# A mixture layer behind a state-space scan on one core: batch 0's output projection, norm and routing moved into batch 1's scan, expert weights loaded by expert

## The reference

```
h = layernorm(x) * (1 + ca) + sa
x = x + ga * (mamba(h) @ Wout.T + bout)       # 512 channels, 16 states each
h = layernorm(x) * (1 + cb) + sb
x = x + gb * moe(h)                           # 8 experts, the 2 best of each token

# mamba, for each channel, state and time step:
hs = exp(delta * A) * hs + (delta * u) * B
y  = sum over the 16 states of hs * C;  y = (y + u * D) * silu(z)
# moe, for each token and each of its two experts:
out += weight * (silu(h @ w0[e]) * (h @ w1[e])) @ wo[e]
```

## Time and profile before

| | us |
|---|---|
| median of three runs | 856.41 (855.0 to 859.22) |
| the profiled execution, its own time | 857.02 |
| its span, first to last instruction | 855.1 |
| TensorE busy | 736.4 (86%) |
| DVE busy | 637.4 (75%) |
| GpSimd busy | 512.8 (60%) |
| ACT busy | 329.6 (39%) |

### The profile page before, as it was taken

The page is one execution under the profiler, slowest core; times in us unless marked ns, Lnnn a source line. Parts: engine busy times, 40 slices in busy tenths (PEclk is TensorE's granted clock), DMA queues, the critical chain, the costliest instruction groups (busy, mean ns, idle before and its releaser), DMA issues. The chain is left out here.

```text
span 855.1 us, 10146 instructions
## 1 busy us (share of the span) xinstructions
PE 736.4 (86%) x2245; PEld 362.4 (42%) x2246; DVE 637.4 (75%) x880; ACT 329.6 (39%) x364; POOL 512.8 (60%) x266
## 2 busy tenths in 40 slices
PE   5899998878888878879788887896499999999994
PEld 3444343222233322323233332575256666666663
DVE  4478899999999999999899998577435445445442
ACT  1786956456454545445354444011111111111110
POOL 1013234999999999899999999546522222222222
PEclk9999999999999999989999899997699999999998
DMA  9354645867668577567689898196323322322220
GB/s 291 99 144 154 206 153 146 207 172 190 178 158 212 158 187 196 160 172 188 171 198 249 217 232 212 56 382 247 105 71 61 50 38 40 49 43 41 46 29 0
DMA packets 61731, 126.33 MB, mean 148 GB/s; under 512 B 11338, under 2 KB 33290, under 8 KB 61580
## 3 DMA queue, kind: packets, MB, share of 16 engines
q1 hardware_dynamic: 49908, 116.12, 49.2%
q0 software_dynamic: 7152, 8.48, 5.6%
q10 hardware_dynamic: 4648, 1.48, 0.7%
HBM read 98.08 MB, written 24.69 MB: 144 GB/s over the span
## 5 line engine op out<-in xcount | busy, mean ns | idle before, releaser
L1450 POOL TENSOR_TENSOR pool<-pool,hT 128x1024 f32<-128x1024 f32 x128 | 298.8, 2357 | 23.0 <-PE PS L619 23.0
L619 PE MATMUL PS<-pool,ident 128*128 128x512 f32 x512 | 267.8, 648 | 44.9 <-POOL pool L1450 43.7
L907 ACT ACTIVATE PS<-pool,negA 128x1024 f32 (+1 forms) x128 | 143.1, 1118 | 188.2 <-DVE pool L1167 188.2
L619 PEld LDWEIGHTS PS<-pool,ident 128*128 128x128 f32 x512 | 95.9, 200 | 158.8 <-POOL pool L1450 81.4
L1520 POOL DMA_INDIRECT out<-uT,ptab x39 | 60.5, 1552 | 168.1 <-DVE uT L1396 161.5
L741 PE MATMUL PS<-pool,uT 128*128 (+1 forms) x312 | 143.5, 603 | 0.6 <-issue 0.6
L1167 DVE TENSOR_TENSOR_SCAN pool<-PS,pool 128x1024 f32<-128x1024 f32 x64 | 142.9, 2272 | 0.4 <-ACT PS L907 0.4
L601 PE MATMUL PS<-pool 96*128 96x512 bf16 x256 | 79.6, 393 | 23.4 <-DVE wz_sb L1155 13.4
L1370 DVE TENSOR_TENSOR uT<-uT,PS 128x512 f32<-128x512 f32 x39 | 26.9, 689 | 88.3 <-PE PS L741 85.5
L1167 DVE TENSOR_TENSOR_SCAN pool<-PS,spread 128x1024 f32<-128x1024 f32 x32 | 73.1, 2284 | 13.2 <-POOL spread L1470 8.9
L1470 POOL TENSOR_TENSOR spread<-spread,pool 128x1024 f32<-128x1024 f32 x32 | 75.4, 2356 | 12.4 <-ACT spread L913 12.4
(11 more groups left out here) (176 smaller groups left out, 782.5 us busy)
## 6 DMA issues: line engine op xcount, KB each, us to landing
hT<-C_scratch SPq DMA_DIRECT2D x128, 512.0 KB, 5.3
pool<-in_w SPq DMA_DIRECT2D x16, 512.0 KB
uT<-expert_in_scratch SPq DMA_DIRECT2D x39, 130.5 KB
Y<-Y SPq DMA_DIRECT2D x32, 128.0 KB, 2.4
C_scratch<-Y SPq DMA_DIRECT2D x8, 512.0 KB, 2.6
pool<-du_scratch SPq DMA_DIRECT2D x8, 512.0 KB, 6.0
Y<-in_wo SPq DMA_DIRECT2D x8, 512.0 KB
expert_in_scratch<-zrow SPq DMA_DIRECT2D x16, 130.5 KB, 5.6
```

What stands on the lines that cost most here:

```text
L619: m = pe.matmul(PS[:, 6 + half, :], ident[:, :], prod[:, k % PR, HF * half:HF * half + HF], start=False, stop=k == DS - 1)
L907: act.activation(pair(2 * (k % 2)).unsqueeze(1), delta[:, bass.ds(g2 * 2 + r, 1), :], ACT.Exp, scale=decay[:, bass.ds(g2 * (2 * DS) + n, 1 ...
L1450: gp.tensor_tensor(prod[:, k % PR, :], hst[:, k % HR, :], crep[k % RC], ALU.mult).then_inc(prod_done, 1)
```

## The change

- **Batch 0 inside batch 1's scan.** The last two pairs of chunks are written out on all engines. In chunk 5 TensorE runs the projection of tiles 0 to 3 in steps 0 to 3, where its `back` stood, and in chunk 6 that of tiles 4 to 7 (`blocks_behind`); the `back`s follow from step 4, two and one in turn. The projection uses the PSUM pair of the sums, and a fifth matmul adds x itself. ACT takes the tile out in steps 4 to 7 (`take_x2`), DVE measures it behind the scans of steps 7 to 10 (`among_scans`), GpSimd computes the power and the shift behind step 11, ACT normalises (`normal_x2`), TensorE turns tiles forward and back in steps 0 to 4 of chunk 7, and ACT scales and shifts them there and copies the rows (`take_turned`, `take_rows2`). The gate logits of the eight tiles stand ahead of the last three `back`s.
- **Products.** From step 72 of 128 the ring of products has `PW` = 6 buffers.
- **Routing groups.** They are eight tiles, four and four. Batch 0 is one group, picked straight behind the last scan.
- **Loads.** w1 of experts 4 to 6 is loaded in the last pair of chunks. Behind the scan the order is w0, w1, wo of one expert after the other, and TensorE waits for the weights of two experts at a time. Batch 0's part of x is stored in chunk 7.
- **First slots.** TensorE's first eight slots are written out, with the expert as a constant.

```diff
-NQ = 4
-TQ = NT // NQ
+TQ = 4
+GROUPS = ((0, NTB), (NTB, NTB + TQ), (NTB + TQ, NT))
+NQ = len(GROUPS)
+S1 = NG // 2 * DS
+RING = S1 + 8
...
+PW = 6
...
+        prods = [prod[:, 0, :], prod[:, 1, :], delta[:, CH - 1 + NG // 2, :], szT[:, 1, :], szT[:, 2, :], szT[:, 3, :]]
...
+        def prod_at(n):
+            return prods[n % PR] if n < RING else prods[(n - RING) % PW]
...
-                        if last and k in (3, 7, 11):
-                            w0_of(3 * r + k // 4)
+                        if last and (r, k) in ((0, 3), (0, 7), (1, 7)):
+                            w1_early(CH + 2 * r + k // 4 - r)
+                        if last and r == 1 and k == 5:
+                            x2_stored(slice(0, NTB))
...
-            for e in range(NE):
-                sp.dma_start(w1_sb[:, e], w1[e].rearrange("(k p) n -> p k n", p=P)).then_inc(w01_in, 16)
+            sp.wait_ge(gated, NG - 1)
+            for e in range(NE - 1):
+                w0_of(e)
+                if e < CH:
+                    w1_of(e)
+                wo_of(e)
+            w0_of(NE - 1)
+            w1_of(NE - 1)
             sp.wait_ge(gated, NG)
-            for e in range(NE):
-                sp.dma_start(wo_sb[:, e], wo[e].rearrange("(k p) n -> p k n", p=P)).then_inc(wo_in, 16)
-            for q in range(NQ):
-                tiles = slice(TQ * q, TQ * q + TQ)
-                sp.wait_ge(x2_step, TQ * q + TQ)
-                sp.dma_start(out_dram[:, tiles, :], x_tok[:, tiles, :]).then_inc(x2_out, 16)
+            wo_of(NE - 1)
+            x2_stored(slice(NTB, NTB + TQ))
+            x2_stored(slice(NTB + TQ, NT))
...
-            for q in range(NQ // 2):
-                sp.wait_ge(sent[q], 16 * 2 * TQ)
+            sp.wait_ge(sent[0], 16 * 2 * NTB)
...
+                if t in (0, TQ):
+                    pe.wait_ge(yev_done, 1 + CH + 1 + t // TQ)
+                elif t < NTB:
+                    if t % TQ >= 2:
+                        pe.wait_ge(x2_step, t - 1)
+                elif t == NTB:
+                    pe.wait_ge(scan_done, 2 + NG * DS)
                     pe.wait_ge(gated, CH * NB)
-                if t >= 6:
+                elif t >= NTB + TQ:
                     pe.wait_ge(x2_step, t - 3)
                 for k in range(CH):
                     m = pe.matmul(PS[:, o_bank(t), 0:DM], uT[:, b * CH + k, at:at + P], (wout0, wout_sb)[b][:, k, :],
-                                  start=k == 0, stop=k == CH - 1)
+                                  start=k == 0, stop=k == CH - 1 and b == 1)
+                if b == 0:
+                    m = pe.matmul(PS[:, o_bank(t), 0:DM], ident[:, :], x_tok[:, t, :], start=False, stop=True)
                 m.then_inc(o_mm, 1)
...
+            def turned_in(j):
+                pe.wait_ge(xn2_done, 2 * j + 2)
+                if j:
+                    pe.wait_ge(t1_done, 2 * j)
+                else:
+                    pe.wait_ge(yev_done, NG)
...
+            def turned_back(j):
+                pe.wait_ge(t1_done, 2 * j + 2)
+                if j:
+                    pe.wait_ge(t2_done, j)
+                else:
+                    pe.wait_ge(yev_done, NG)
...
+            def first_logits(tiles):
+                for t in tiles:
+                    if t == 0:
+                        pe.wait_ge(dbu_done, 1 + NG * OWN)
+                        pe.wait_ge(spread_in, NG * len(SHARED))
+                        pe.wait_ge(t1_done, NTB)
+                    for k in range(KD):
+                        m = pe.matmul(PS[:, 4, NE * t:NE * t + NE], h2T[:, t, k, :], gate_sb[:, k, :],
+                                      start=k == 0, stop=k == KD - 1)
...
+            def pair_read(g):
+                if g == CH + 3:
+                    pe.wait_ge(t1_done, NTB)
+                    pe.wait_ge(t2_done, NTB // 2)
+                elif g > CH:
+                    pe.wait_ge(x2_step, TQ * (g - CH))
+
+            def blocks_behind(g2, r, pieces, last):
+                made = 0
+                for k in range(DS):
+                    next_front(g2, r, k, last)
+                    if k < len(pieces):
+                        pieces[k]()
+                        continue
+                    for _ in range(min(2 - (k - len(pieces)) % 2, k + 1 - made)):
+                        if last and made >= DS - 3:
+                            first_logits(range(3 * (made - DS + 3), min(3 * (made - DS + 3) + 3, NTB)))
+                        if made == 0:
+                            pair_read(2 * g2 + r)
+                        back(g2, r, made, prod_at(DS * (2 * g2 + r) + made))
+                        made += 1
...
-            blocks_of(NG // 2 - 1, True)
+            with pe.Fori(0, NB) as g2:
+                blocks_of(g2)
+            blocks_behind(NB, 0, [], False)
+            blocks_behind(NB, 1, [lambda t=t: outward_y(t) for t in range(TQ)], False)
+            blocks_behind(NB + 1, 0, [lambda t=t: outward_y(t) for t in range(TQ, NTB)], False)
+
+            def turned_pairs(j):
+                if j:
+                    turned_back(j - 1)
+                if j < NTB // 2:
+                    turned_in(j)
+
+            blocks_behind(NB + 1, 1, [lambda j=j: turned_pairs(j) for j in range(NTB // 2 + 1)], True)
...
+            ranks(0)
+            for t in range(NTB, NT):
+                outward_y(t)
+            for q in range(1, NQ):
                 scored(q)
-                if q == 0:
-                    outward_y(TQ + 2)
-                elif q == 1:
-                    outward_y(3 * TQ)
                 ranks(q)
...
             pe.wait_ge(x2_step, NT)
-            pe.wait_ge(w01_in, 16 * 2 * NE)
-            pe.wait_ge(wo_in, 16 * NE)
...
+            for s2 in range(NE // 2):
+                for r in range(2):
+                    following = 2 * s2 + r + 1
+                    turn(s2 + 1, r)
+                    turn_inter(s2, r)
+                    if following == NE:
+                        pe.wait_ge(c_over, 1)
+                    hidden(s2 + r, 1 - r, following if following < NE else None)
...
+            def take_x2(t):
+                act.wait_ge(o_mm, t + 1)
+                act.activation(x_tok[:, t, :], PS[:, o_bank(t), 0:DM], ACT.Copy).then_inc(x2_step, 1)
+
+            def normal_x2(t):
+                act.wait_ge(nmr_done, 2 * (t // TQ) + 2)
...
+                act.activation(xn2[t // TQ][:, t % TQ, :], x_tok[:, t, :], ACT.Identity,
+                               bias=nmr[:, t:t + 1], scale=rstd[:, t:t + 1]).then_inc(xn2_done, 1)
+
+            def take_turned(j):
+                act.wait_ge(t1_mm, j + 1)
...
+                for k in range(KD):
+                    act.activation(h2T[:, 2 * j:2 * j + 2, k, :], PS[:, 6, 2 * P * k:2 * P * k + 2 * P].rearrange("p (t n) -> p t n", t=2),
+                                   ACT.Identity, bias=h2c[:, 1, k:k + 1], scale=h2c[:, 0, k:k + 1]).then_inc(t1_done, 1)
+
+            def take_rows2(j):
+                act.wait_ge(t2_mm, j + 1)
+                act.activation(h2row[:, 2 * j:2 * j + 2, 0:DM], PS[:, 7, :].rearrange("p (t n) -> p t n", t=2), ACT.Copy).then_inc(t2_done, 1)
+
+            def among_decays(g, k):
+                if g in (CH + 1, CH + 2) and k in range(LAG, LAG + TQ):
+                    take_x2(TQ * (g - CH - 1) + k - LAG)
+                if g == CH + 2 and k in range(LAG + TQ, LAG + 2 * TQ):
+                    normal_x2(k - LAG - TQ)
+                if g == CH + 3:
+                    if k < TQ:
+                        normal_x2(TQ + k)
+                    if k in range(LAG, LAG + NTB // 2):
+                        take_turned(k - LAG)
+                    if k in range(LAG + 1, LAG + 1 + NTB // 2):
+                        take_rows2(k - LAG - 1)
...
+            def among_scans(g, k):
+                if g in (CH + 1, CH + 2) and k in range(LAG + 3, LAG + 3 + TQ):
+                    first = TQ * (g - CH - 1)
+                    measured(first + k - LAG - 3)
+                    if k == LAG + 2 + TQ:
+                        for t in range(first, first + TQ):
+                            gathered(t)
...
-            residual(0)
-            route_tables()
-            normal_h2(0)
+            pick(0)
             gate_y(NG - 1)
-            for t in (TQ, TQ + 1):
-                added_y(t)
-            for t in (TQ, TQ + 1):
-                measured(t)
-            pick(0)
             weights(0)
             place_of(0)
-            added_y(TQ + 2)
-            added_y(TQ + 3)
-            measured(TQ + 2)
-            measured(TQ + 3)
-            for t in range(TQ, 2 * TQ):
-                gathered(t)
+            step(dve.tensor_copy(ef[:, 0:NE], iota8[:, :]))
+            step(dve.tensor_copy(etab[:, 0:NE], iota8[:, :]))
+            residual(1)
             normal_h2(1)
-            for q in range(1, NQ):
-                if q < NQ - 1:
-                    residual(q + 1)
-                pick(q)
-                weights(q)
-                place_of(q)
```

(38 more changed lines are left out.)

388 lines of the change are left out of this document (219 added, 169 removed).

## The result

The changed kernel takes 850.03 us (median of 13 runs, 846.69 to 854.32) against 857.37 for the kernel before, run beside it (13 runs, 855.0 to 863.21). The ratio is 0.990 [0.9878, 0.9923]: faster by 1.0% (7 to 10 us), where 19 us were forecast. The profiled execution took 852.29 us, with a span of 850.5. In it the last recurrence ends at 553.62 us (forecast 544) and the second slot's hidden product starts at 616.11 (forecast 600).

What follows compares the result with a forecast made beforehand. DVE was taken to bound the scan, GpSimd just under it, and TensorE the experts. The 79.35 us between shrink to 55.9, gaining 23.4, less 4.5 in the scan: 857.02 - 18.9 gives 838 us, range 829 to 850.

Steps and rivals of the forecast that it cites:

- start and chunks 0 to 4: Scan before the projection: early constants and four small loads at the start were to cost nothing, 0 us.
- chunks 5 and 6, projection in lumps: Scan: projection and added engine work, partly hidden by fronts and six product buffers, costs 1.9 us for each chunk.
- chunk 7, turns ahead of the backs: Last scan chunk: first back waits for ACT's last copied rows, 3.6 us late, but the chunk pays only 0.7 us.
- E to batch 0 placed (logits ahead of the last backs): From the last recurrence's end (E) through batch 0's logits, ranks and places: 11.4 us.
- from there to the last ranks done: Routing behind the scan, from batch 0 placed at 11.4 to the last group ranked at 41.3 us after the last recurrence.
- pause ahead of the places: Last routing group: half of 6.5 us of unexplained ACT and DVE idle time was expected to remain, 3.2 us.
- places to the second slot's product: Start of the experts: first turn at 41.5 us, then 11.2 us to the second slot's hidden product, as before.
- from there to the end: Experts from the second slot's hidden product on: TensorE is the bound and 238.0 us are carried over unchanged.
- The logits: Behind the scan: batch 0's logits stand ahead of the last back and are ready 4.2 us after the last recurrence.
- The last gate: Behind the scan: last product, its back, ACT's leave and DVE's gate end 9.1 us after the last recurrence.
- The powers behind the sends: GpSimd behind the scan: batch 1's powers queue behind 13 sends, the second ready 31.1 us after the last recurrence.
- the chain of transfers is later than the routing: Rival, chance 0.17: behind the scan, batch 0's sends and first slot's rows land late; some 8 us, total 846.

Runs made afterwards that it cites:

- e1: Changed kernel with batch 0's turns and logits moved behind the scan, projection kept in chunks 5 and 6; 859.36 us, ratio 1.0024 to the kernel before.
- e9: Changed kernel with batch 0's turns back to rows and ACT's double rows behind the last back, turns inward over two banks, two taken a step; 839.79 us, ratio 0.9896.
- f3: As e9, but the four turns inward over one bank and ACT taking one a step; 842.48 us, ratio 0.9841 to the kernel before.
- f1: The changed kernel unaltered, run again on another chip; 847.78 us, ratio 0.9897 to the kernel before.
- e8: Changed kernel with only half of group 1's sends moved behind group 2's; 848.64 us, ratio 0.9899 to the kernel before.
- e5: e4 with batch 1's powers behind 4 and 8 of batch 0's sends in place of 8 and 13; 853.91 us, ratio 0.9948 to the kernel before.
- f4: f2 with batch 1's powers behind 4 and 8 sends and the weights of experts 5 to 7 late; 844.28 us, ratio 0.9880 to the kernel before.
- e4: Changed kernel with the weights of experts 5 to 7 issued behind the fetches of slots 1 to 3; 852.48 us, ratio 0.9957 to the kernel before.
- f2: The kernel of e9 run again, on the same chip as f1; 842.62 us, ratio 0.9830 to the kernel before.
- e6: e4 with half of group 1's sends moved behind group 2's; 847.58 us, ratio 0.9910 to the kernel before.
- e7: Changed kernel with ACT taking rows first, late weights of experts 5 to 7, powers behind 4 and 8 sends, half of group 1's sends late; 847.37 us, ratio 0.9875.
- g1: e9 with half of group 1's sends moved behind group 2's; 840.98 us, ratio 0.9799 to the kernel before.
- g2: g1 with the weights of experts 5 to 7 also issued late; 840.36 us, ratio 0.9791 to the kernel before.

## Why the prediction was wrong

The direction was right and the size was not: 838 forecast, 850.03 measured, just outside the range (829 to 850). Of the profiled execution, 852.3 against the sum's 838.1:

| term | forecast | trace | difference |
|---|---|---|---|
| start and chunks 0 to 4 | 0 | 3.9 | +3.9 |
| chunks 5 and 6, projection in lumps | 3.8 | 0.4 | -3.4 |
| chunk 7, turns ahead of the backs | 0.7 | 9.7 | +9.0 |
| E to batch 0 placed (logits ahead of the last backs) | 11.4 | 14.9 | +3.5 |
| from there to the last ranks done | 29.9 | 31.9 | +2.0 |
| pause ahead of the places | 3.2 | 5.3 | +2.1 |
| places to the second slot's product | 11.4 | 10.4 | -1.0 |
| from there to the end | 238.0 | 236.2 | -1.8 |

**The step that failed is the price of chunk 7**: "In chunk 7 it waits for ACT's last copied rows and comes 3.6 us late", and 0.7 us taken for it. GpSimd's wait for that back was 9.48 us, and the chunk's price 9.7. The mechanism was named, its length was not worked out. I gave ACT's copies a price of nothing because half of ACT's time was free (and counted 16 turned halves where there are 8), and TensorE's turns 0.60 for four; I never laid the copies and the turns end to end. They alternate: 1.09 + 1.06 + 1.02 + 0.59, less the overlaps, 3.63 us a link, and with the slower first steps they put the first back 18.3 us behind the first turn. e1 (48.8 us without them), e9 (51.4) and f3 (52.5) show it, and with them GpSimd's wait for the first back: 9.48 us in the changed kernel, 3.66 in f3, 2.48 in e9, 0.67 in e1. The half clock was not in the forecast either. It is 0.84 us of each link at half clock, and f1 and e8 against the changed kernel put 2.5 of the 9.7 us on what it costs behind the first back. Why it lasts longer in some traces of the same scan is open.

**Chunks 5 and 6** were overpriced: I charged for work added to full engines (3.8 us), and the ring of six covered it, all but 0.90 us of GpSimd's time a chunk. e1 and the changed kernel agree on 51.5 and 51.6.

**The logits** were left out of the path. They stand between the last backs, 1.40 + 1.40 + 0.95 = 3.75 us for 32 matmuls of eight columns, 0.117 us each, and the last back waits for them. No run moved them alone, so this term rests on the timeline. The last gate, which the prediction puts at 9.1 us though its four pieces add up to 8.4, came at 12.8 behind the same backs.

**The powers behind the sends** came as forecast, some 4 us later, as all behind the logits did. Shortening that wait gained nothing: in e5 and f4 the places came 1.4 and 1.7 us later (against e4 and f2), because late signals took its place. What it would give without late signals was not run.

**The pause** was forecast at half of the 6.5 us read before and was 5.3 from rank to places. What arrives late is TensorE's signal, with a run of sends going on; why, is open. The Trainium skill (Runtime: NRT & Kernel Launch, section Instruction fetch mechanics) says that in straight code the fetch of the next block is mostly hidden; the traces agree as far as they go, since the last rank's matmul has started 5 us before DVE sees its signal, and the same code of the routing runs without the pause in e9.

**The rival "the chain of transfers is later than the routing"** had the right sign at the first turn (6.87 us of waiting for rows) and a total (846) nearer to the 850 measured. The second is luck: e4 removed the wait and gained nothing, and e8 shows that these rows bind only where the pause is gone.

**Start and chunks 0 to 4** have the same work in both kernels. Chunk 5 begins at 387.29 in the one trace of before, at 391.20 in the changed kernel, and between 386.96 and 393.60 in the other traces of its kind: a spread wider than the difference. No run settles whether part of the 3.9 us is the change's. So 3.9 of the 14 us are not explained. The median lies 2.3 us below the profiled execution.

No slot is seen waiting for weights, as forecast.

## What to carry to other kernels

Free time of an engine says nothing of a chain in which two engines hand pieces to each other: lay one link end to end, multiply, and ask who is locked out until the last. Work that is put ahead of a ring's consumer has to be shorter than what the ring holds; move the part that nobody needs yet (here the turns to rows) behind the loop. Compare two versions of a stretch by more than one trace each, and look at the granted clock first: here the same scan took 58.0 or 60.6 us. And before a late transfer is priced, look for what the next stage waits for when it is early: the first turn came 6.7 us earlier here and the end did not.

## What the runs showed of the chip

- On four of five chips, signals of TensorE's finished matmuls to ACT and DVE came 2 to 7 us late while GpSimd's indirect sends ran on without a break; in e5 a signal of DVE to itself was 1.7 us late as well. In nine traces the one ahead of the places arrived 1.4 to 1.7 us behind the last send of the run (2.2 in e5; in the kernel before DVE's came 0.65 behind), and the later ones of e6, e7, e8, g1 and g2 0.7 to 2.2 us behind the run of twelve. But others arrived 2 to 3 us late with the sends still going on (two in e5, one in e7, ACT's at 600.63 in the kernel before), so the end of the run is not what always sets them free. On the fifth chip the one trace with a run of sixteen (e9) has none, and the kernel before was 4 to 8 us faster there than on the others. The cause is open, and so is whether the profiling takes part in it.
- TensorE's granted clock fell to half (0.5, 1.2 of 2.4 GHz) at 503.1, behind the first four turns and in a wait of 1.62 us for DVE's drive. It stayed there through the chain of short turns and waits for ACT, and rose again at 523.6, 4.3 us into the first backs, which stand without a pause.
- With transfers at a share of 1.06 (575 to 600 us) and 0.98 (599.52 to 607.30), a fetch of 130.5 KB issued at 599.52 was there at 607.3 (7.7 us; the shortest landing on this tensor before is 2.2), and it had been issued 6.2 us behind the end of the sixteenth send (before 2.8).
